# Other byte offsets for the split activations of a mixture-of-experts kernel on one Trainium2 core

## What is computed

```python
def reference(x, log_A, B_w, B_b, C_w, C_b, Wr, br, W1, W3, W2):
    xn = layernorm(x)
    B_x = einsum('btd,nd->btn', xn, B_w) + B_b
    h = scan(h_t = sigmoid(log_A) * h_(t-1) + B_x_t)
    s = einsum('btn,dn->btd', h, C_w) + C_b
    logits = einsum('bsh,he->bse', xn, Wr) + br
    top, which = top_k(logits, 2); c = one-hot sum of softmax(top)
    gate = einsum('bsh,ehi->besi', xn, W1)
    up   = einsum('bsh,ehi->besi', xn, W3)
    y    = einsum('besi,eih->besh', silu(gate) * up, W2)
    g    = silu(einsum('bse,besh->bsh', c, y))
    return x + s * g
```

## Time and profile before

| | us |
|---|---|
| median of 3 runs | 791.45 |
| lowest, highest | 791.40, 793.32 |
| the profiled execution, its time | 792.44 |
| its span, first to last instruction | 790.7 |
| TensorE busy | 765.4 (97%) |
| VectorE busy | 518.5 (66%) |
| GpSimd busy | 464.8 (59%) |
| ScalarE busy | 376.2 (48%) |
| granted TensorE clock, mean | 0.995 |

### The profile page before, as it was taken

How to read it: one execution, slowest core, us unless ns; L and a number is a source line. 1 busy time by engine, 2 the same in 40 slices (tenths; PEclk the granted TensorE clock), 3 DMA queues, 4 the chain that set the end, 5 groups by cost and what they waited for, 6 DMA issues and landing times.

```text
span 790.7 us, 17130 instructions
## 1 busy us (share of the span) xinstructions
PE 765.4 (97%) x5399; PEld 683.5 (86%) x5399; DVE 518.5 (66%) x1083; ACT 376.2 (48%) x667; POOL 464.8 (59%) x477
## 2 busy tenths in 40 slices
PE   4999989999999999999999999999999999999997
PEld 2554449999999999999999999999999999998786
DVE  6988975776778657666866664555656765542766
ACT  3985234544455445445544554445546644442530
POOL 4742847687577667845783686468557856554000
PEclk9999999999999999999999999999999999999999
DMA  9999813544565444425643644264537554943994
GB/s 291 336 314 322 138 39 110 136 73 67 134 134 113 100 97 97 67 49 140 141 68 93 167 67 75 42 142 67 112 68 200 97 131 96 330 70 41 315 372 164
DMA packets 101842, 111.02 MB, mean 140 GB/s; under 512 B 15634, under 2 KB 89236, under 8 KB 101748
## 3 DMA queue, kind: packets, MB, share of 16 engines
q0 software_dynamic: 25920, 35.54, 27.3%
q1 hardware_dynamic: 50032, 50.34, 20.2%
q10 hardware_dynamic: 25796, 24.20, 10.7%
HBM read 66.61 MB, written 43.45 MB: 139 GB/s over the span
## 4 chain that ended last, share of the span: by engine, by line
PE 87%; DVE 7%; DMA 2%; issue 2%; ACT 1%; POOL 0%; ACTq 0%; DVEq 0%; POOLq 0%; SPq 0%
PE bank L1538 15%; PE bank L1512 15%; PE bank L1513 15%; PE bank L1514 15%; PE bank L1539 7%; PE bank L1646 6%; PE bank L1412 4%; DVE xnT L1090 2%; PE bank L1500 2%; DVE stats L961 1%; PE bank L1375 1%; PE bank L1564 1%; PE bank L1565 1%; PE bank L1563 1%; PE bank L1642 1%
## 5 line engine op out<-in xcount | busy, mean ns | idle before, releaser
L609 POOL DMA_INDIRECT y_rows<-y_sb,token_at x128 | 214.6, 1677 | 143.1 <-DVE y_sb L1208 73.3
L1512 PE MATMUL bank<-xh,W_sb 128*128 128x256 f32 x1008 | 283.2, 281 | 0.1
L1514 PE MATMUL bank<-xl,W_sb 128*128 128x256 f32 x1008 | 281.8, 280 | 0.0
L1513 PE MATMUL bank<-xh,W_sb 128*128 128x256 f32 x1008 | 281.7, 279 | 0.0
L1512 PEld LDWEIGHTS bank<-xh,W_sb 128*128 128x128 f32 x1008 | 189.2, 188 | 2.3 <-DVE xl L1156 0.4
L1513 PEld LDWEIGHTS bank<-xh,W_sb 128*128 128x128 f32 x1008 | 189.3, 188 | 0.0
L1514 PEld LDWEIGHTS bank<-xl,W_sb 128*128 128x128 f32 x1008 | 189.0, 188 | 0.0
L1538 PE MATMUL bank<-W_sb,hh 128*128 128x512 f32 x512 | 187.7, 405 | 1.0 <-DVE y_sb L1208 0.9
L1196 DVE TENSOR_TENSOR hbuf<-hbuf,bank 128x512 f32<-128x512 f32 x128 | 87.5, 687 | 153.5 <-PE bank L1514 149.0
L600 POOL DMA_INDIRECT xg<-xn_rows,token_at x128 | 144.9, 1132 | 38.3 <-issue 18.6
L1539 PE MATMUL bank<-W_sb,hl 128*128 128x256 f32 x512 | 143.8, 281 | 0.0
(11 more groups left out here) (255 smaller groups left out, 921.7 us busy)
## 6 DMA issues: line engine op xcount, KB each, us to landing
x_late<-L_attn_x SPq DMA_DIRECT2D x24, 512.0 KB, 9.2
raw<-L_ffn_W ACTq DMA_DIRECT2D x24, 512.0 KB, 4.3
odd_raw<-L_ffn_W ACTq DMA_DIRECT2D x21, 512.0 KB
xn_rows<-h_sb SPq DMA_DIRECT2D x16, 512.0 KB, 6.5
y_rows<-xnT SPq DMA_DIRECT2D x4, 2048.0 KB, 15.7
yy<-y_rows SPq DMA_DIRECT2D x16, 512.0 KB, 9.3
out<-x_late SPq DMA_DIRECT2D x11, 512.0 KB, 6.6
x_kept<-L_attn_x SPq DMA_DIRECT2D x4, 512.0 KB, 6.8
```

The costliest lines, as they stand in the source:

```text
L609: return eng.indirect_dma_start(out=y_rows, out_offset=rows, in_=y, in_offset=None, bounds_check=T + TW - 1, oob_is_err=True, compute_op=A ...
L1512: eng.matmul(part, high, x_h, start=k == 0, stop=False)
L1513: eng.matmul(part, low, x_h, start=False, stop=False)
L1514: last = eng.matmul(part, high, x_l, start=False, stop=k == KD - 1)
```

## The change

The four tensors `xh`, `xl`, `hh` and `hl` become slices of one tensor `parts` of 5360 words, at byte 200160 (480 modulo 512). `hbuf` moves in front of it, and `ident_r` ahead of `w_slot`, which puts `ident_r` at 416 modulo 512. `W_sb`, `xg`, `odd_W` and all the odd tiles' tensors stay where they are.

- `xh` and `xl` begin 32 and 672 words into `parts`, both at 96 modulo 512, and their second row block follows 288 words after the first instead of 256. So the first block (k = 0) stands 192 bytes past the weights modulo 512, the second (k = 1) 320.
- `hh` begins at word 1232 and `hl` at word 3296, and the second buffer of each follows 1040 words after the first. Past the weights modulo 512: `hh` 384 and 448 (r = 0 and 1), `hl` 448 and 512, which is 0.
- The reads and writes of x's parts become patterns of two blocks of 256 columns in place of one run of 512. The count and the order of instructions on each engine, and all waits, are the same as before.

```diff
@@ the tensors of the middle
             xg = sb("xg", [P, XG_RING, 2, ROW], f32, mid)
-            xh = sb("xh", [P, KD * TW], f32r, mid)
-            xl = sb("xl", [P, KD * TW], f32r, mid)
             hbuf = sb("hbuf", [P, KI * TW], f32, mid)
-            hh = sb("hh", [P, 2, KI * TW], f32r, mid)
-            hl = sb("hl", [P, 2, KI * TW], f32r, mid)
+            parts = sb("parts", [P, 5360], f32r, mid)
             y_sb = sb("y_sb", [P, Y_RING, 2, D], f32, mid)
             y_low = sb("y_low", [P, 2, D], f32, mid)
+            ident_r = sb("ident_r", [P, P], f32r, mid)
             w_slot = sb("w_slot", [P, SLOT_TILES], f32, mid)
-            ident_r = sb("ident_r", [P, P], f32r, mid)
...
-        first_xh, first_xl = (odd_W[:, n * KD * TW:(n + 1) * KD * TW] for n in range(2))
+        X_STEP, H_STEP = 288, 1040
+        def x_part(at):
+            return parts[:, at:at + KD * X_STEP].rearrange("p (k n) -> p k n", k=KD)[:, :, 0:TW]
+        def h_part(at):
+            return [parts[:, at + r * H_STEP:at + r * H_STEP + KI * TW] for r in range(2)]
+        xh, xl = x_part(32), x_part(672)
+        hh, hl = h_part(1232), h_part(3296)
+        first_xh, first_xl = (odd_W[:, n * KD * TW:(n + 1) * KD * TW].rearrange("p (k n) -> p k n", k=KD) for n in range(2))
@@ x_high (ScalarE)
-                eng.activation(to[:, :], ps_xT[:, :], ACT.Copy).then_inc(xh_ready, 1)
+                eng.activation(to, ps_xT[:, :].rearrange("p (k n) -> p k n", k=KD), ACT.Copy).then_inc(xh_ready, 1)
@@ h_high (ScalarE)
-                eng.activation(hh[:, r, n * 512:(n + 1) * 512], hbuf[:, n * 512:(n + 1) * 512], ACT.Copy).then_inc(hh_ready, 1)
+                eng.activation(hh[r][:, n * 512:(n + 1) * 512], hbuf[:, n * 512:(n + 1) * 512], ACT.Copy).then_inc(hh_ready, 1)
@@ x_low (VectorE)
-                eng.tensor_tensor(low[:, :], ps_xT[:, :], high[:, :].bitcast(f32), ALU.subtract).then_inc(xl_ready, 1)
+                eng.tensor_tensor(low, ps_xT[:, :].rearrange("p (k n) -> p k n", k=KD), high.bitcast(f32), ALU.subtract).then_inc(xl_ready, 1)
@@ product (TensorE)
-                        x_h, x_l = high_x[:, k * TW:(k + 1) * TW], low_x[:, k * TW:(k + 1) * TW]
+                        x_h, x_l = high_x[:, k, :], low_x[:, k, :]
@@ down (TensorE); h_low (VectorE) likewise
-                        h_h, h_l = (h[:, r, k * TW + t * P:k * TW + (t + 1) * P] for h in (hh, hl))
+                        h_h, h_l = (h[r][:, k * TW + t * P:k * TW + (t + 1) * P] for h in (hh, hl))
```

More of the change, by code:

```diff
@@ L1200, in h_low @@
                 eng.wait_ge(hh_ready, 2 * i + (n + 1))
-                eng.tensor_tensor(hl[:, r, cols], hbuf[:, cols], hh[:, r, cols].bitcast(f32), ALU.subtract).then_inc(hl_ready, 1)
+                eng.tensor_tensor(hl[r][:, cols], hbuf[:, cols], hh[r][:, cols].bitcast(f32), ALU.subtract).then_inc(hl_ready, 1)
             def add_y(i, r, stored):
```

## The result

The changed kernel takes 784.91 us in the median of 5 runs (784.61 to 786.56), the one before 791.45 (789.66 to 793.32, 5 runs). The ratio is 0.9911, with a 95% interval of 0.9895 to 0.9928: 0.7 to 1.1% faster, about 7 us. The forecast was 779.0 in a range of 760 to 799. Its direction was right, its size nearly double.

What follows compares the result with a forecast made beforehand. TensorE's matmul pace was taken as the bound. The terms, -12.7 + 0 + 0.3 + 0 = -12.4 us, set against the median of 791.45, gave 779.0 us, range 760 to 799, the forecast's own 772 to 786.

Steps and rivals of the forecast that it cites:

- What bounds the kernel: Whole kernel: TensorE, busy 97% of the span; time is the number of matmuls times their pace.
- Term 1: Gate and up, 3024 matmuls: x's parts farther from the weights, 113.7 ns each, 4.2 less; -12.7 us.
- Term 2: `down`, 512 pairs: h's new offsets change nothing, 353 ns a pair stays; 0, bounds 5.1 us either way.
- Term 3: The 256 transposes: `ident_r` moves to the same offset as `xg`, costing +0.3 us.
- Term 4: x_high and x_low writing 2 x 256 columns: cost covered, 0; up to 0.32 us a step at most.
- No effect past 64 bytes: Product matmuls: 64 bytes already brought all there is; time 791.5 us, chance 0.22.
- Slower, by the alternation: Product: separation jumping between 192 and 320 bytes makes every matmul cost 120.0 ns; 798.2 us, chance 0.24.
- All of the excess goes: Product: new offsets keep the two reads apart, matmuls run at 108 ns; 761.9 us, chance 0.12.

Runs made afterwards that it cites:

- i1_x192_h_after: Against the kernel before: both row blocks of x at 192, h's parts at 384/448 and 448/0 as in the changed kernel; 784.34 us, ratio 0.9900.
- e2_h_alone: Against the kernel before: only h's parts moved, to 384/448 (buffer 0) and 448/0 (buffer 1), x's parts all at 64; 786.07 us, ratio 0.9934.

## Why the prediction was right in direction and wrong in size

**What bounds the kernel**: right. A change of 1 ns in a matmul's pace is 3 us at the end, and the middle shortened with the paces.

**Term 1, x's parts (-12.7 us)** is the step that failed, in size and in mechanism. Product went from 117.8 to 116.9 ns by its steady paces, -2.8 us by 3024 matmuls, and from first to last start all gates and ups together became only 1.7 us shorter, since waits and first distances came on top. x alone measured 0.19 to 0.37%, 1.5 to 2.9 us. "64 bytes brought 2.1 ns, so 192 bring 6.3" had two points and laid a line through them. The pattern repeats after 256 bytes, so k = 1 at 320 stayed where it had been at 64, and k = 0 at 192 is as far from a multiple of 256 as 64 is, on the other side, and allows the same two paces. With the same h it took the quick one more often, in 29 steps (i1_x192_h_after) against 16 (e2_h_alone); why, stays open. The value that I wrote down for a matmul, 113.7, is close to the 113.3 that does occur, but it occurs at 64 too, where by the slope it could not. "Its pace is that of every step", the prediction says of the kernel before; one gate of the 63, step 1's, ran at 113.3, and reading all of them would have shown that 64 bytes had a second pace.

**Term 2, h's parts (0, bounds of 5.1 us either way)** is mis-sized: 353 became 347 and 340 ns a pair, 256 x 6 + 256 x 13 = 4.9 us by the steady paces, 3.2 us over whole `down`s, whose first pairs are slower; h alone measured 0.53 to 0.80%, 4.2 to 6.3 us, of which 3.1 are the 16 product steps that became quick. The value lay in the bound that the earlier trace rows gave. I had read these rows as a disturbance ahead of the steady state. They were the steady state's alternative: 343 ns showed that a pair can be quicker at the same addresses, and it should have been a case of its own.

**So the direction was in part luck.** Of the 12.7 us of term 1 at most 2.8 came, 1.7 from start to start, and the larger part of the gain, 3.2 us, came from `down`, which the sum had at nothing. That the time fell within the forecast's own 772 to 786 us is a small part of term 1 and an unforeseen term 2, with about 1 us of the measured difference due to the clock.

**Term 3, the transposes (+0.3 us)**: not seen. Four took 0.29 to 0.30 us in both profiles. **Term 4, patterns of two blocks (0)**: right, and cheaper than its bound. ScalarE's and VectorE's instructions for x's parts after (groups, 120 to 710 us), for the earlier trace rows:

```profile
L802 ACT ACTIVATE parts<-bank 128x512 fp32r<-128x512 f32 x63 | 37.6, 597 | 21.5 <-PE bank L1509 17.5 <-remote 2.8 <-issue 1.1
L1165 DVE TENSOR_TENSOR parts<-bank,parts 128x512 fp32r<-128x512 f32 x63 | 43.5, 691 | 19.3 <-ACT parts L802 15.6 <-issue 3.7
```

597 and 691 ns, to the nanosecond what one run of 512 columns took the earlier trace rows.

**The rivals.** "No effect past 64 bytes" is out: h alone is faster by 0.66% and 256 bytes slower by 0.4%. Its observation about the pairs was right, and it spoke against the reading (two reads that meet) on which term 1 stood; I noted it and did not use it. The Trainium skill's sentence that the next load doesn't steal bandwidth from a running matmul ("TensorE: Matmul & The Clock Gate", section "Step-by-step: what each phase is for") fits the halved loads and doesn't cover the rest: operand offsets alone moved this kernel's time from 0.9879 to 1.0041 of the one before. "Slower, by the alternation" did not come: the mixture has a pace of its own, 116.7, between the 113.3 and 117.8 of its blocks alone. "All of the excess goes" did not come in any kernel; no steady pace below 113.3 was seen.

**Not foreseen at all** was the clock: some 3 of the 7.5 us of difference between the two profiles, in places that the change doesn't touch.

## What to carry to other kernels

Where one long stream of matmuls is the bound, read its pace from the distances of starts, step by step, before and after: a mean hides that it is made of two or three values. Operand offsets are then worth a sweep, by steps of 32 or 64 bytes and not by a slope, and each part's best value has to be measured together with the others, since moving h changed the pace of x's matmuls. A time that comes out as forecast doesn't prove its terms; compare them one by one. Compare runs with equal granted clock where a gain of less than 1% is at stake.

## What the runs showed of the hardware

- Matmuls of 256 float32r columns in a stream keep one of a few paces, 113.3, 116.7, 117.8, 118.3, 118.7 or 120.0 ns, for a whole gate and up if nothing interrupts them, and the same addresses can have two of them (113.3 and 117.8 at 64, 192, 320 and 448 bytes). Behind a break between gate and up, with starts 0.15 to 0.48 us apart, the `up` took another pace in some steps. Pairs of 512 and 256 columns keep 340, 347, 350 or 353 ns.
- The pace depends on the difference of the addresses of what moves and what is loaded, modulo 256 bytes: moving it by 256 reproduced 27 steps in a row, moving both by 160 left 54 of 62 product steps and every `down` as they were.
- Loads of 64 columns instead of 128, 134 ns instead of 188, beside the same streams gave 117.4 ns in place of 117.8.
- Behind an idle time of about 2 us TensorE's granted clock fell to 1.2 GHz in some executions and not in others, behind 2.13 and 1.89 us in one profile and not behind 2.06 and 2.17 in the other. From the end of the idle time on, each fall cost about 1.7 us.
